# Local attention of a four-layer transformer kernel: score products of 32 partitions, values as stationary operand, output turned beside the probabilities, and two unused full products per unit

## What is computed

```python
qkv = (xw @ W_qkv).reshape(B * nw, WINDOW, 3, NUM_HEADS, HEAD_DIM)   # windows of 64 tokens, 16 heads of 8
q, k, v = (qkv[:, :, 0], qkv[:, :, 1], qkv[:, :, 2])
q = _layernorm(q, ln_gamma, ln_beta)
k = _layernorm(k, ln_gamma, ln_beta)
attn = jnp.einsum('bqhd,bkhd->bhqk', q * SCALE, k)                   # SCALE is 1
attn = jax.nn.softmax(attn, axis=-1)
out = jnp.einsum('bhqk,bkhd->bqhd', attn, v).reshape(B * nw, WINDOW, C)
out = out @ W_proj + b_proj
```

## Time and profile before

| | us |
|---|---|
| median of 3 runs (lowest, highest) | 892.42 (891.72, 892.43) |
| profiled execution, its time | 885.71 |
| its span | 883.9 |
| PE, DVE, ACT, POOL busy | 731.3, 686.8, 570.6, 394.5 |
| mean granted TensorE clock, share of full | 0.903 |

### The profile page before, as it was taken

How to read it: one execution, slowest core, us unless ns; L and a number is a source line. 1 busy time by engine, 2 the same in 40 slices (tenths; PEclk the granted TensorE clock), 3 DMA queues, 4 the chain that set the end, 5 groups by cost and what they waited for, 6 DMA issues and landing times. The chain is left out here.

```text
span 883.9 us, 11015 instructions
## 1 busy us (share of the span) xinstructions
PE 731.3 (83%) x3306; PEld 469.4 (53%) x3306; DVE 686.8 (78%) x1615; ACT 570.6 (65%) x926; POOL 394.5 (45%) x427
## 2 busy tenths in 40 slices
PE   4788998779998889999778988877778767877787
PEld 3666765445555567777566867643223222222565
DVE  6685786798998638777767888968899778786785
ACT  5264664657474435664636767667899879777776
POOL 6638665634345105555329977534323332230330
PEclk9999998988697669999969999987899889789999
DMA  4200000100000000000001000000000000000001
GB/s 134 72 12 13 16 16 18 34 24 25 13 25 19 0 1 1 1 1 0 1 0 37 1 1 0 1 0 1 1 0 1 1 1 0 1 0 1 1 1 48
DMA packets 9610, 11.59 MB, mean 13 GB/s; under 512 B 720, under 2 KB 5712, under 8 KB 9552
## 3 DMA queue, kind: packets, MB, share of 16 engines
q1 hardware_dynamic: 9552, 10.89, 4.3%
HBM read 9.84 MB, written 1.05 MB: 12 GB/s over the span
## 5 line engine op out<-in xcount | busy, mean ns | idle before, releaser
L1032 POOL TENSOR_TENSOR rbuf<-B,rbuf 128x512 fp32r<-128x512 f32 x96 | 124.1, 1295 | 83.6 <-ACT rbuf L960 83.4
L497 POOL TENSOR_SCALAR small<-small 128x4 f32<-128x4 f32 x32 | 8.5, 265 | 173.3 <-DVE small L387 172.8
L994 DVE TENSOR_TENSOR B<-B,up_banks 128x512 f32<-128x512 f32 x68 | 46.4, 683 | 42.3 <-PE up_banks L733 25.8
L945 ACT ACTIVATE B<-gate_banks 128x512 f32<-128x512 f32 x68 | 40.6, 599 | 59.4 <-PE gate_banks L733 58.3
L960 ACT ACTIVATE rbuf<-B 128x512 fp32r<-128x512 f32 x100 | 62.5, 625 | 17.3 <-DVE B L1010 12.3
L1010 DVE TENSOR_TENSOR B<-B,spread_bank 128x512 f32<-128x512 f32 x96 | 64.7, 678 | 11.0 <-ACT B L949 7.0
L1757 ACT ACTIVATE B<-B,VEC 128x1024 f32<-128x1024 f32 x48 | 55.3, 1151 | 22.4 <-DVE B L1752 22.3
L731 PE MATMUL gate_banks<-XH,WH 128*128 128x512 f32 x152 | 67.0, 441 | 0.8 <-ACT YT L1355 0.8
L733 PE MATMUL gate_banks<-XH,WL 128*128 128x512 f32 x152 | 62.4, 410 | 0.0
L732 PE MATMUL gate_banks<-XL,WH 128*128 128x512 f32 x152 | 62.3, 410 | 0.0
L949 ACT ACTIVATE B<-gate_banks,WR 128x512 f32<-128x512 f32 x64 | 44.0, 689 | 27.3 <-PE gate_banks L733 26.7
(11 more groups left out here) (347 smaller groups left out, 2274.3 us busy)
## 6 DMA issues: line engine op xcount, KB each, us to landing
STG<-in_w_split SPq DMA_DIRECT2D x27, 256.0 KB, 2.7
X<-in_x SPq DMA_DIRECT2D x4, 256.0 KB, 5.0
out<-X SPq DMA_DIRECT2D x4, 256.0 KB, 2.3
WR<-in_w_raw SPq DMA_DIRECT2D x1, 524.5 KB, 4.4
STG<-in_w_exact SPq DMA_DIRECT2D x2, 256.0 KB, 2.6
STG<-in_w_split SPq DMA_DIRECT2D x5, 64.0 KB, 1.9
STG<-in_w_split SPq DMA_DIRECT2D x1, 192.0 KB, 2.4
STG<-in_w_split SPq DMA_DIRECT2D x1, 128.0 KB, 2.0
```

The lines of the kernel that those rows point to most:

```text
L994: nc.vector.tensor_tensor(MO[n % 2], AO[n % 2], U[n % 2][:, :], ALU.mult).then_inc(mul_done, 1)
L1032: e_.tensor_tensor(lo, hidden(f, n), hi.bitcast(F32), ALU.subtract).then_inc(hl_ready, 1)
```

## The change

- **Keys.** The features of four heads fill 32 partitions. `KM` now holds four copies of the chunk's keys, one per place of a head in its group of four, with the other three places set to 0. They are made once per chunk, straight from the normalized keys with scale and offset (`attn_keys`): two of 128x512 by ACT, two by POOL, none by DVE. Two small vectors for this are made by POOL beside later weights. The masks per tile and the scaled keys `KN` go.
- **Scores.** A unit takes four products, one per window and group of four heads, each of 32 rows by 64 columns and moving 256 columns (`attn_scores`). The two groups write different banks. They wait for the keys at a chunk's first unit and, instead of for DVE's read, for ACT's evacuation of the unit two back (`pt_ready`), because probabilities are now turned back into the same banks. Ahead of them, from unit 2 on, stand two products of 512 columns with full weights into these banks, whose result nobody reads and the next products overwrite. The scores of units 0 and 1 move into the feed-forward layer ahead, in front of its last two products.
- **Weighing.** The values are stationary (18 columns for two heads), the probabilities move (64 columns): eight products over four column tiles of 32. The output has features on the partitions, so ACT copies it (`copy_out`), PE turns it two units later, next to the probabilities of the same bank pair (`turn_out`), and the evacuation takes both (640 columns instead of 512). DVE's finish works on that, per unit.
- **Statistics.** The squares are stationary, so that the sums have tokens on the partitions; root and reciprocal are 128x128 instead of 32x512. ACT spreads the reciprocals to 512 columns (`attn_spread_act`), and four products with the identity per q and k turn them.
- **Order.** Weighing now stands ahead of the scores on PE; on ACT the evacuation and the copy stand ahead of the exponential. Preparation moves to steps 0, 1, 2, 4 and 5.

```diff
                     down(*at_)
+                    if f is FFN0 and at_ == (NC - 1, f.blocks - 3):
+                        for N in range(2):
+                            attn_scores(pe, N)
...
-        PREPARE_AT = {1: 0, 2: 1, 3: 2, 5: 3}
+        PREPARE_AT = {0: (0,), 1: (1,), 2: (2,), 4: (4,), 5: (5, 3)}
...
+                for j in range(TL):
+                    for sq, name, at_ in ((sqq, "mean_q", 0), (sqk, "mean_k", NH)):
+                        i = nc.tensor.matmul(R[:, j * GR + at_:j * GR + at_ + NH], sq[:, j * P:(j + 1) * P],
+                                             raw(name, at_, NH), start=True, stop=True)
+                i.then_inc(var_full, 1)
...
+            if step in (4, 5):
+                pe.wait_ge(rstd_wide, 2 * c + step - 3)
+                if step == 5:
+                    pe.wait_ge(qk_read, 2 * c + 1)
+                for j in range(TL):
+                    i = nc.tensor.matmul(R[:, j * P:(j + 1) * P], (sqq, QN[c % 2])[step - 4][:, j * P:(j + 1) * P],
+                                         ident, start=True, stop=True)
+                i.then_inc(rstd_full, 1)
...
+        def attn_spread_act(a, c):
+
+            a.wait_ge(rstd_qk, c + 1)
+            if c >= 2:
+                a.wait_ge(s_full, UN * (c - 1))
+            for dst, at_ in ((sqq, NH), (QN[c % 2], 0)):
+                nc.scalar.activation(dst.rearrange("p (t h d) -> p t h d", t=TL, d=HD),
+                                     bcast(rstd.rearrange("p (t h) -> p t h", t=TL)[:, :, at_:at_ + NH].unsqueeze(3),
+                                           [P, TL, NH, HD]), ACT.Copy).then_inc(rstd_wide, 1)
...
+            if step in (4, 5):
+                k, x = step - 4, (kc, qc)[step - 4]
+                v.wait_ge(rstd_full, 2 * c + k + 1)
+                v.wait_ge(centred, 2 * c + 2)
+                nc.vector.tensor_tensor(x, x, R[:, :], ALU.mult).then_inc(qk_read, 1)
+            if step == 5:
+                v.wait_ge(qk_read, 2 * c + 2)
+                if c >= 2:
+                    v.wait_ge(s_full, UN * (c - 1))
+                nc.vector.tensor_scalar(QN[c % 2], qc, raw("ln_g1"), raw("ln_b1"), ALU.mult, ALU.add)\
+                    .then_inc(qk_ready, 1)
...
+            for j in ((0, 1) if eng is nc.scalar else (2, 3)):
+                dst = KM[c % 2][:, j, :]
                 if eng is nc.scalar:
-                    i = eng.activation(dst, src, ACT.Copy, scale=raw("head_mask", h, 1))
+                    i = eng.activation(dst, kc, ACT.Identity, scale=key_g[:, j:j + 1], bias=key_b[:, j:j + 1])
...
-                    i = eng.tensor_scalar(dst, src, raw("head_mask", h, 1), None, ALU.mult)
-            i.then_inc(done, 1)
+                    i = eng.tensor_scalar(dst, kc, key_g[:, j:j + 1], key_b[:, j:j + 1], ALU.mult, ALU.add)
...
+        def attn_scores(pe, N):
...
+            if N % UN == 0:
+                pe.wait_ge(keys_act, c + 1)
+                pe.wait_ge(keys_pool, c + 1)
+                pe.wait_ge(qk_ready, c + 1)
+            if N >= 2:
+                pe.wait_ge(pt_ready, N - 1)
+            else:
+                pe.wait_ge(act_done, NC * FFN0.blocks)
+                pe.wait_ge(mul_done, NC * FFN0.blocks)
+            if N >= 2:
+                for k in range(2):
+                    nc.tensor.matmul(SBW[u][:, k, :], wh("wv1")[0], chunk(XH, c, PAD), start=True, stop=True)
+            for w in range(2):
+                tok = slice(i_ * P + w * WIN, i_ * P + (w + 1) * WIN)
+                for k in range(2):
+                    rows = slice(32 * (2 * u + k), 32 * (2 * u + k) + 32)
+                    i = nc.tensor.matmul(SB2[u][w * WIN:(w + 1) * WIN, k, :], QN[c % 2][rows, tok],
+                                         KM[c % 2][rows, :, tok], start=True, stop=True)
+            i.then_inc(s_full, 1)
...
+            def turn_out(M):
+                u = M % 2
+                pe.wait_ge(o_copied, M + 1)
+                for k in range(2):
+                    rows = slice(64 * k, 64 * k + 64)
+                    i = nc.tensor.transpose(SBW[u][:, k, HALF:TURN_W], OT[u][rows, :], ident[rows, rows])
+                i.then_inc(o_turned, 1)
...
             def turn(N):
...
                 if N >= 2:
-                    pe.wait_ge(pt_ready, N - 1)
+                    turn_out(N - 2)
                 for q in range(4):
-                    i = nc.tensor.transpose(U[u][:, q * P:(q + 1) * P], PRB[u][:, q * P:(q + 1) * P], ident)
+                    i = nc.tensor.transpose(SB2[u][:, q // 2, q % 2 * P:(q % 2 + 1) * P],
+                                            PRB[u][:, q * P:(q + 1) * P], ident)
                 i.then_inc(p_turned, 1)
...
+                if N:
+                    pe.wait_ge(o_copied, N)
+                for w in range(2):
+                    for q in range(4):
+                        at_ = q % 2 * P + w * WIN
+                        i = nc.tensor.matmul(SP[32 * q:32 * q + 2 * (HD + 1), u * P + w * WIN:u * P + (w + 1) * WIN],
+                                             VB[:, tile % TL, 4 * u + q, w, :, :].rearrange("p h d -> p (h d)"),
+                                             PT[u][:, q // 2, at_:at_ + WIN], start=True, stop=True)
                 i.then_inc(o_full, 1)
...
                 if N:
                     turn(N - 1)
-                scores(N + 1)
                 if N >= 2:
                     weigh(N - 2)
+                if N:
+                    attn_scores(pe, N + 1)
...
+                if nxt:
+                    for step in PREPARE_AT.get(n, ()):
+                        if step != 3:
+                            attn_prepare_pe(pe, c + 1, step)
                 if n == 3 and c:
                     attn_turn_pe(pe, c - 1)
                 if n == 4 and c:
                     attn_project_pe(pe, c - 1)
-                attn_hooks(n, c, hook, 4)
-                if n in PREPARE_AT and nxt:
-                    attn_prepare_pe(pe, c + 1, PREPARE_AT[n])
+                attn_hooks(n, c, hook, 5)
+                if nxt and n == 5:
+                    attn_prepare_pe(pe, c + 1, 3)
...
+                a.wait_ge(o_full, N - 1)
+                if N >= 4:
+                    a.wait_ge(o_read, N - 3)
+                nc.scalar.activation(PT[N % 2], SBW[N % 2][:, :, 0:TURN_W], ACT.Copy).then_inc(pt_ready, 1)
...
+            def copy_out(N):
+                u = N % 2
+                a.wait_ge(o_full, N + 1)
...
+                    a.wait_ge(o_turned, N - 1)
+                nc.scalar.activation(OT[u], SP[:, u * P:(u + 1) * P], ACT.Copy).then_inc(o_copied, 1)
...
                 N = c * UN + n
-                probs(N)
                 if N:
                     evac(N - 1)
-                if n == 1:
+                if N >= 2:
+                    copy_out(N - 2)
+                probs(N)
+                if n == 0:
                     attn_values_act(a, c, 1)
...
+                if n == 3 and nxt:
+                    attn_spread_act(a, c + 1)
...
+                if n == 5 and nxt:
+                    attn_keys(nc.scalar, c + 1)
...
+            def finish(M):
+
+                v.wait_ge(pt_ready, M + 3)
...
+                chain(nc.vector.reciprocal(rec_.rearrange("p (k q h) -> p k q h", k=2, q=2), O[:, :, :, HD::HD + 1]))
+                for k in range(2):
+                    i = nc.vector.tensor_tensor(
+                        AT[c_ % 2][:, i_ * P + u * WIN + k * 32:i_ * P + u * WIN + (k + 1) * 32]
...
+                if nxt and n == 3:
+                    attn_prepare_dve(v, c + 1, 2)
+                if nxt and n == 4:
                     attn_prepare_dve(v, c + 1, 4)
-                if u == 0:
-                    if N >= 4:
-                        finish(N // 2 - 2)
-                    attn_mask(nc.vector, N // 2 + 1)
+                if nxt and n == 5:
+                    attn_prepare_dve(v, c + 1, 5)
...
+                if N >= 4:
+                    finish(N - 4)
...
+                if n == 5:
+                    attn_keys(nc.gpsimd, c + 1)
...
```

More of the change, by code:

```diff
@@ L659, in later_weights @@
         def later_weights(g, chain):
+            for row, dst in (("ln_g1", key_g), ("ln_b1", key_b)):
+                i = nc.gpsimd.tensor_scalar(dst, raw("head_of_4"), raw(row), 1.0, ALU.mult, ALU.mult)
+            chain(i)
             WM32 = buf[11]
@@ L1114, in attn_early_pe @@
                 pe.wait_ge(piece_ready, READY_AT["wv1"])
-            if b != 4:
-                if b < 7:
-                    attn_prepare_pe(pe, 0, b if b < 4 else b - 1)
-                else:
-                    attn_values_pe(pe, 0, 0)
-        def attn_early_act(a, b):
-            if b < 4:
-                attn_prepare_act(a, 0, b)
+            for step in EARLY_AT.get(b, ()):
+                attn_prepare_pe(pe, 0, step)
+            if b == 7:
+                attn_values_pe(pe, 0, 0)
+        def attn_early_act(a, b):
+            for step in EARLY_AT.get(b, ()):
+                attn_prepare_act(a, 0, step)
```

(60 more changed lines are left out.)

157 lines of the change are left out of this document (65 added, 92 removed).

## The result

The changed kernel took 921.62 us (median of 4 runs, 916.64 to 923.16), the kernel before 892.31 us on the same chip: a ratio of 1.032, 95% interval 1.0279 to 1.0361. It is slower by 3.2% where 1.3% faster was forecast, and lies above 897 us, the upper end of the range. The profiled execution took 920.57 us, its span is 918.6 us. Executions more than 1.5% above the fastest of the same kernel count as disturbed and are in no ratio.

The account below looks back on a forecast made before the run. Took DVE and PE, both near full, DVE leading, as the bound. Third to last scores 81.2 + 29 + 14 + 5 = 129 us against 140.1, -11; behind -1; sum -12, median 880.4 us, range 866 to 897.

Parts of the forecast that it names:

- the clock term: Attention stage: 57 us at 1.2 GHz shrink to some 10 us, worth 5 us; bounds nothing or 57 us.
- The rival that named this: Unused products fail to hold the clock: 15 us more, 895 us, kept with the slower case, together 0.22.
- Waits: PE's waits in the attention stage: 0.3 us a unit for ACT's evacuation, plus 14 us of stalls over the chunks.
- The 2.0 us at step 4: PE's projection waits 2.0 us at step 4 for DVE's key product, cast and difference.
- PE per unit: PE's turns, weighing, scores, unused products, waiting and shape changes sum to 2.8 us a unit at 2.4 GHz, against 2.43.
- The rival of tiles that don't overlap: Score tiles of different rows serialize, +0.45 us a unit; with the shape-change case 890 to 904, taken as 895; chance 0.22.
- The extra changes of shape: Three more tile-shape changes per unit on PE, 0.16 us in all; +0.35 us a unit if each costs fully.
- DVE, ACT, POOL: Attention stage: DVE falls from 130 to about 90 us, ACT stays at 90, POOL's key scalings take 1 us each.
- ACT as the bound: ACT's loop of 3.2 us a unit loses 0.4 us a unit to waits, 11.6 us: a tie at 892 us, chance 0.08.
- Front and behind: Up to the third unit's scores 0 us, bounds -3 and +3; from the last scores to the next stage -1 us.

Follow-up runs that it names:

- the lean version: Changed kernel with values placed one step later, projection ahead of preparation, preparation one step later, and no unused products in the units: 888.01 us, 1.0002.
- the 32-row run: Kernel before with its scores contracted over the first 32 of 128 rows, for measuring only: 930.78 us, 1.0466.
- the all-orders version: Changed kernel with values placed one step later, projection ahead of preparation and preparation one step later, unused products kept: 899.86 us, 1.0111.
- the late start: Changed kernel with its first two scores behind the feed-forward layer's last product: 919.78 us, 1.0394.
- the fill products: Four unused 512-column products per chunk in the statistics: 893.97 us, 1.0054 in the all-orders version; 893.86 us, 1.0071 in the lean version.
- masked queries alone: Changed kernel with scores over 128 rows, DVE copying each group's queries into a buffer zero in the other rows: 921.56 us, 1.038.

## Why the prediction was wrong, step by step

**The step that failed is the clock term**: "Those causes go, and each unit gets two full products. I leave one short drop a chunk, some 10 us of low clock in sum worth 5 us." Measured are 113 us of low clock. By the same rule, half of it, they are worth up to 56 us in place of 5; the stage took 171 us in place of 129, 42 us more, while the idle time came out near its forecast. Four things were wrong in the term.
- It named PE's waits and the lack of products as what moves the clock and never asked what a product of 32 rows does to it. In the old kernel's scores that alone takes the clock from 0.81 to 0.57; in the lean version the way back takes it from 0.68 to 0.95. The Trainium skill, "TensorE: Matmul & The Clock Gate", section "What's actually happening", says that the clock follows from how busy PE has been. The row of the 32-row run differs: the records have PE busy 98%, and the clock is 0.57.
- It misread the old trace. That "the drops follow stretches in which PE waited 1.3 to 1.5 us" fits some falls, those at 193 and 271.5 us. The ones at 227.0 and 264.5 us have no such wait ahead of them, but the two spreading products of 32 rows.
- It counted on the unused products. They cost 22.9 us in the stage (0.79 us for each of 29 pairs, where 0.46 was taken at the high clock) and moved the clock by 0.01. The rival that named this put 15 us more on the low clock, 895 us, and was short as well; it was the right sign and the nearest case. That full products can hold clock was not wrong as such: they did in the old kernel (0.904 to 0.915) and a little in the all-orders version (0.68 to 0.74).
- It took the waits at the chunks' starts for small. Moving the one call that made them raised the clock from 0.67 to 0.75.

**Waits.** I put 0.3 us a unit and 14 us of stalls, 23 us in all; idle is 25 us. The sum was right, its place and price were not. "ACT's placing of values (1.12 us) and square and copy (1.2 us) delay the evacuation at steps 0, 1 and 7, about 1.4 us together" missed that the placing waits for a weighing of the next step: PE waits 3.0 us there, and the low clock that follows is dearer. Moving one call gave 17.8 us in the profile's stage and 13 us by the ratios (1.0177 against 1.032). The 2.0 us at step 4 measured 2.39, twice.

**PE per unit.** 2.8 forecast, 2.97 measured at 2.4 GHz. Turn of the output 0.25 and 0.21, weighing 0.5 and 0.42, scores 0.6 and 0.59, products 0.46 and 0.63, wait for the evacuation 0.3 and 0.54. The rival of tiles that don't overlap falls: 0.59 us for eight passes, and 1.02 us once they take 128 rows. The extra changes of shape left no idle time of PE in the rows; no run measures them by themselves.

**DVE, ACT, POOL.** 90, 90 and 1 us a key forecast for 161 to 312 us; measured 87 and 88 over 183 us, and 1.02 a key in the mean (0.76 in the first chunk). Right, and without effect, since neither was the bound any longer. ACT as the bound falls: it is busy 88 of 183 us and waits for PE.

**Front and behind.** 0 within 3 us forecast, 4.2 us later measured: POOL's keys ended at 158.5, not at 156, and PE stood 3.82 us ahead of the first scores with two of the layer's products behind them. With the late start the third scores come at 163.2, better than before. Behind -1 forecast, -2.3 measured.

**What stays open.** Why 32 rows lower the clock is not shown, only that they do, in two kernels; only 32 and 128 rows were tried. Two products a unit cost 5 us in the old kernel, where the clock rose, and 23 in the stage of the new (19 by the ratios), where it did not; why it rose in the one alone is not settled. The same goes for the fill products, which gained 0.6% with the units' products there and lost 0.7% without them. The falls of the all-orders version behind its narrow passes are not explained either: such passes lower nothing in the old kernel. Nor was the kernel before tried with its two spreading products over all rows, which the falls behind them suggest.

## What to carry to other kernels

Row tiles that overlap save time only if the clock holds: here four overlapping 32-row products (0.59 us) lost to the same four over 128 rows, whose row tiles don't overlap (1.02 us), because the clock went from 0.68 to 0.95. Zero rows in the stationary side make such a product correct at the price of small copies, two a unit here. When a kernel runs two clocks, cost each edit at both, and look first for fixed waits by order: one call moved by one step was worth 13 us. Before putting a fall of the clock down to a wait, list what PE ran just ahead of each fall. Removing one of several causes may show nothing (1.038 with masked queries alone) until the others are gone too.

## What the hardware showed that I had not expected

In this kernel the granted clock went with how many rows of the array the products fill: 64 score products over 32 in place of 128 rows, with the same columns, took the stage's clock from 0.81 to 0.57 at 98% busy. Unused 512-column products over 128 rows beside them did little against it: none, two and four a unit gave 0.66, 0.67 and 0.73. In the kernel without 32-row scores two a unit raised the mean clock of whole executions from 0.904 to 0.915. And passes of 16 columns over 128 rows, 1.86 us of them, did not lower it there.
